# A selective-scan layer on one core: the input product of the scan as matmuls with diagonal blocks, and plain additions of y

## What is computed

```
dA  = jnp.exp(dt[..., None] * A)
dBx = (dt * x)[..., None] * Bm[:, :, None, :]
def step(h, inputs):
    dA_t, dBx_t, C_t = inputs
    h = dA_t * h + dBx_t
    y = jnp.einsum('bdn,bn->bd', h, C_t)
    return (h, y)
...
y = ys + x * D
```

## Time and profile before

| | us |
|---|---|
| median of 3 runs | 1387.32 |
| lowest, highest | 1381.39, 1389.28 |
| the profiled execution | 1389.91 |
| its span, first to last instruction | 1388.1 |
| TensorE busy | 1228.0 (88%) |
| VectorE busy | 899.6 (65%) |
| GpSimd busy | 918.5 (66%) |
| ScalarE busy | 777.4 (56%) |

### The profile page before, as it was taken

The page is one execution under the profiler, slowest core; times in us unless marked ns, Lnnn a source line. Parts: engine busy times, 40 slices in busy tenths (PEclk is TensorE's granted clock), DMA queues, the critical chain, the costliest instruction groups (busy, mean ns, idle before and its releaser), DMA issues. The chain is left out here.

```text
span 1388.1 us, 20902 instructions
## 1 busy us (share of the span) xinstructions
PE 1228.0 (88%) x7120; PEld 933.0 (67%) x7120; DVE 899.6 (65%) x1065; ACT 777.4 (56%) x1477; POOL 918.5 (66%) x511
## 2 busy tenths in 40 slices
PE   8978878989788879797787879898999999999997
PEld 3445555656556556566556644467999999999996
DVE  3998999899899899899998889963111111111110
ACT  4787887788887697788886675613111111111111
POOL 1998999999999989999998879822222222222211
PEclk9999999999999899899998799999999999999999
DMA  5665556465556455556555554608988898888982
GB/s 196 216 182 183 168 184 176 156 202 192 176 171 198 152 184 165 183 171 192 186 184 182 178 155 152 194 4 301 369 309 322 318 322 313 310 320 317 323 306 46
DMA packets 109979, 296.95 MB, mean 214 GB/s; under 512 B 10017, under 2 KB 21922, under 8 KB 94386
## 3 DMA queue, kind: packets, MB, share of 16 engines
q1 hardware_dynamic: 100226, 277.53, 57.9%
q0 software_dynamic: 9648, 18.09, 6.5%
HBM read 277.76 MB, written 9.96 MB: 207 GB/s over the span
## 5 line engine op out<-in xcount | busy, mean ns | idle before, releaser
L1376 POOL TENSOR_TENSOR arena<-arena 128x1024 f32<-128x1024 f32 x192 | 456.7, 2395 | 53.8 <-DVE arena L1096 38.2
L472 PE MATMUL ps_y<-ident,arena 128*128 128x128 f32 x1840 | 258.5, 289 | 54.0 <-POOL arena L1376 53.3
L472 PEld LDWEIGHTS ps_y<-ident,arena 128*128 128x128 f32 x1840 | 222.2, 148 | 121.8 <-POOL arena L1376 74.3
L1428 POOL DMA_INDIRECT out_x<-arena x39 | 61.8, 1585 | 304.9 <-ACT arena L1024 279.8
L871 ACT ACTIVATE arena<-arena,An 128x512 f32<-128x512 f32 x316 | 218.6, 710 | 0.1
L871 ACT ACTIVATE ps_de<-arena,An 128x512 f32<-128x512 f32 x196 | 134.9, 688 | 146.4 <-DVE arena L1083 140.4
L1310 DVE TENSOR_TENSOR arena<-ps_du,arena 128x512 f32<-128x512 f32 x39 | 27.0, 692 | 227.8 <-PE ps_du L720 227.8
L1360 POOL TENSOR_TENSOR arena<-arena 128x1024 f32<-128x1024 f32 x67 | 160.2, 2391 | 6.7 <-DMA arena<-bc_scratch 6.7
L720 PE MATMUL ps_y<-arena 128*128 128x128 f32 x1248 | 153.4, 276 | 0.8 <-ACT arena L1012 0.5
L720 PEld LDWEIGHTS ps_y<-arena 128*128 128x128 f32 x1248 | 149.6, 193 | 3.2 <-ACT arena L1012 0.8
L1068 DVE TENSOR_TENSOR ps_u<-ps_du,arena 128x512 f32<-128x512 f32 x196 | 136.8, 698 | 22.2 <-DVE arena L1108 10.1
(11 more groups left out here) (238 smaller groups left out, 2009.2 us busy)
## 6 DMA issues: line engine op xcount, KB each, us to landing
arena<-bc_scratch SPq DMA_DIRECT2D x256, 512.0 KB, 4.7
arena<-in_W SPq DMA_DIRECT2D x117, 1024.0 KB
arena<-arena POOLq DMA_DIRECT2D x15, 512.0 KB, 6.0
arena<-in_cd SPq DMA_DIRECT2D x16, 256.0 KB, 5.4
out_x<-arena SPq DMA_DIRECT2D x17, 128.0 KB, 5.0
arena<-in_xT SPq DMA_DIRECT2D x2, 1024.0 KB, 6.3
arena<-in_w2c SPq DMA_DIRECT2D x1, 2048.0 KB, 9.2
diag<-in_dd SPq DMA_DIRECT2D x16, 128.0 KB, 5.1
```

The costliest lines, as they stand in the source:

```text
L472: t = e.matmul(Y[j][:, part], src[:, part], ident[:, :], start=False, stop=stop, is_transpose=True, skip_group_check=True)
L1376: e.tensor_tensor(hc[:, i % NP, :, :], hh[:, i % NH, :, :], c, ALU.mult).then_inc(gp_hc, 1)
L1428: e.indirect_dma_start(out, bass.IndirectOffsetOnAxis(dest[:, i:i + 1], 0), yo[:, i % 3, :], None, compute_op=ALU.add).then_inc(l_add, 16)
```

## The change

From unit 16 on, the input u of both scans is made by TensorE alone. For each unit the 512 values of B[n] are laid out as four diagonal blocks of 128x128; a product of the transposed du (stationary) with such a block (moving) gives du · B in PSUM, where both scans read it. The diagonals are built in a DRAM scratch: it is zeroed once (16 transfers), and for each half sequence four transfers write single elements at a stride of 513. Then the loads of B read the blocks (256 KB a unit, as the spread rows did). Decays then all go to SBUF. In the first 16 units u is made as before by VectorE and GpSimd, now in all of them. Own units become 3, 7, 11 and 15 of the first 16, and 4, 12, 20 and 28 of each 32 after. All additions to Y become matmuls of 128x512 against the identity, and with them the products with D and of the forward direction; nothing is turned back. The ring of three pairs becomes six buffers for B and six for C. Slots of the side work are moved by some units.

```diff
-OWN = (6, 9, 12, 15, 22, 25, 28, 31)
-NR, NH, NP, KD, LAG, EV, NW = 3, 5, 4, 6, 2, 4, 3
+FIRST = 16
+OWN_FIRST, OWN = (3, 7, 11, 15), (4, 12, 20, 28)
+NRB, NRC, NH, NP, KD, LAG, EV, NW = 6, 6, 5, 4, 6, 2, 4, 3
...
+DU_AT = {16 * g - 5 + j + (3 if g == 1 else g == 7): (g, j) for g in range(1, 16) for j in range(2)}
+SCATTER_AT = {i_: (0, 0, k) for k, i_ in enumerate((7, 8, 9, 10))}
+SCATTER_AT |= {22 + k: (0, 1, k) for k in range(4)}
+SCATTER_AT |= {32 * c_ - 12 + 2 * k: (c_ // 2, c_ % 2, k) for c_ in range(2, 2 * NQ) for k in range(4)}
+ZERO_AT = {i_: (c_, 2 * k) for c_ in range(2) for k, i_ in enumerate(range(12 * c_, 12 * c_ + 8))}
...
+        S = [[DU, DE[0]], [U, DE[1]]]
...
                 for j in range(2):
-                    t = add_blocks(q, th, j, hc[:, i % NP, j, :], n == 15)
+                    t = e.matmul(Y[j][:, :], ident[:, :], hc[:, i % NP, j, :], start=False, stop=(n == 15))
                 t.then_inc(pe_y, 1)
...
+            def make_u(i):
+                g, k_ = i // 16, i - 2
+                if i == FIRST:
+                    e.wait_ge(dv_u, FIRST)
+                e.wait_ge(dv_sA, k_ + 1)
+                e.wait_ge(dv_sB, k_ + 1)
+                if own(k_):
+                    e.wait_ge(dv_hc, owned(k_))
+                for j in range(2):
+                    is_free(("du", g, j))
+                rb_has(e, i)
+                for j in range(2):
+                    for k in range(4):
+                        t = e.matmul(S[i % 2][j][:, QUARTERS[k]], duT[:, g % 2, k, j * 128:j * 128 + 128],
+                                     rb[:, i % NRB, QUARTERS[k]], start=True, stop=True)
+                t.then_inc(pe_u, 1)
 
             for i in range(NU + LAG):
-                if i + 1 in DU_AT:
-                    turn_inputs(i + 1)
...
+                if FIRST <= i < NU - 2:
+                    if i == FIRST:
+                        make_u(i)
+                        make_u(i + 1)
+                    make_u(i + 2)
                 if i < NU:
                     side_work(i)
...
-                decay, x = (h[:, 1, :], DE[i % 2][:, :]) if flipped(i) else (DE[i % 2][:, :], h[:, 1, :])
+                decay, x = (DE[i % 2][:, :], h[:, 1, :]) if i < FIRST else (h[:, 1, :], S[i % 2][1][:, :])
...
+            def load_b(i):
...
+                if i < FIRST:
+                    src = bc_dram[0:1, n, HB[0]].to_broadcast([128, TH])
+                else:
+                    src = dg_dram[th, n, 0:128 * TH].rearrange("(p t) -> p t", t=TH)
+                e.dma_start(rb[:, i % NRB, :], src).then_inc(l_rb[i % NRB], 16)
...
+            def put_diagonals(q, th, k):
...
+                to = dg_dram[th].rearrange("n (p f) -> n p f", f=TH + 1)[:, :, k * 128]
+                src = xd[RK:RK + NS, th * TH + k * 128:th * TH + k * 128 + 128]
+                e.dma_start(to, src, allow_slow_non_contiguous=True).then_inc(l_dg, 16)
...
             for i in range(NU):
...
-                if not flipped(i):
+                if i < FIRST:
                     u(i)
...
-                if swapped(i):
-                    first_scan(i)
-                    second_scan(i)
-                else:
-                    second_scan(i)
-                    first_scan(i)
+                second_scan(i)
+                first_scan(i)
```

More of the change, by code:

```diff
@@ L73 @@
+TILE_AT = {at(2, 46): (0, 4), at(2, 47): (0, 5), at(2, 54): (0, 6), at(2, 55): (0, 7),
+           at(3, 6): (0, 0), at(3, 7): (0, 1), at(3, 14): (0, 2), at(3, 15): (0, 3),
+           at(3, 46): (1, 4), at(3, 47): (1, 5), at(3, 51): (1, 6), at(3, 52): (1, 7)}
 TILES = list(TILE_AT.values()) + [(1, i) for i in range(4)]
 TILE_NO = {x: k for k, x in enumerate(TILES)}
[L77 to L84, removed]
@@ L87, in plain @@
[L87 to L104, removed]
+DU_AT = {16 * g - 5 + j + (3 if g == 1 else g == 7): (g, j) for g in range(1, 16) for j in range(2)}
+CD_AT = {(slots[2 * m] - 4 if m < 2 else slots[2 * m - 3] + 7): (q_, m) for q_, slots in CONV_SLOTS.items() for m in range(4)}
@@ L253, in build @@
         pe_D, ac_ev = (sem(n) for n in ("D", "ev"))
-        ac_yT, pe_back = sem("yT"), sem("back")
-        pe_dT, pe_bT, ac_uT, pe_u1, pe_u0, ac_kept = (sem(n) for n in ("dT", "bT", "uT", "pu1", "pu0", "kept"))
+        pe_u = sem("pu")
         ac_z = sem("z")
@@ L283, in own, with rb_has, rc_has, made @@
         def own(i):
-            return i % 32 in OWN
+            return i in OWN_FIRST if i < FIRST else i % 32 in OWN
         def owned(i):
-            return i // 32 * len(OWN) + sum(k <= i % 32 for k in OWN)
+            return sum(own(k) for k in range(i + 1))
+        def rb_has(e, i):
+            e.wait_ge(l_rb[i % NRB], 16 * (i // NRB + 1))
+        def rc_has(e, i):
+            e.wait_ge(l_rcs[i % NRC], 16 * (i // NRC + 1))
+        def made(i):
+            return i - FIRST + 1
+        def cd_of(q, m):
+            return duT[:, 1, :, :].rearrange("p k (a f) -> p k a f", a=2)[:, :, m % 2, :] if q == 0 and m >= 2 else cdiag[:, m % 2, :, :]
+        def du_of(g):
+            return du1 if g == 1 else duA
         def cols_of(q, th):
@@ L458, in tile_lg @@
                 e.matmul(PS[p][:, 0:E], ones_r, bgr, start=False, stop=True).then_inc(pe_lg, 1)
[L460 to L474, removed]
             def first_sum(i, j):
@@ L480, in first_sum @@
                     qe, the, pre, _ = unit(i - 16)
-                    if turned(qe, the):
+                    if qe == 3 and the:
+                        e.wait_ge(dv_lg, 2 * pre + j + 1)
+                    else:
                         e.wait_ge(ac_ev, nth_sum(qe, the, 2 * pre + j))
-                    else:
-                        e.wait_ge(dv_lg, 2 * pre + j + 1)
                 e.wait_ge(l_D, 16 * (i // 16 + 1))
                 has_x(e, q, m, th)
[L487 to L493, removed]
+                e.matmul(Y[j][:, :], diag[:, j, :], xc[q % 2][:, m, HB[th]], start=True, stop=False).then_inc(pe_D, 1)
             def add(i):
                 q, th, pr, n = unit(i)
-                if n == 0 and i >= 16 and turned(*unit(i - 16)[:2]):
-                    turn_back(i)
                 for j in range(2):
@@ L613, in second_u @@
[L613 to L622, removed]
-                    e.wait_ge(dv_hc, owned(i - 1))
-                for k in range(4):
-                    t = e.transpose(U[:, QUARTERS[k]], uT[:, k, 0:128], ident[:, :])
-                t.then_inc(pe_u0, 1)
@@ L897, in evac_turned @@
                     is_full(e, ("wb", NB - 1))
+                    if pr:
+                        for j in range(2):
+                            is_full(e, ("du", 1, j))
                 elif q == 2:
```

317 lines of the change are left out of this document (150 added, 167 removed).

## The result

| | before | after |
|---|---|---|
| median, us | 1384.36 | 1781.42 |
| lowest to highest, us | 1381.12 to 1389.28 | 1780.01 to 1787.78 |
| span of the profiled execution, us | 1388.1 | 1778.1 |
| last addition to y ends, us | 915.75 | 1308.43 |
| behind it, us | 472.3 | 469.7 |

The ratio is 1.287, with an interval of 1.282 to 1.293. The kernel is slower by 397 us. Of the 390.0 us between the two profiled spans, all lies ahead of the last addition (392.7 us later); the part behind it is the same within 3 us. The forecast was 1722 us in a range of 1690 to 1810; the time lies in the range, 59 us above the forecast.

The account below looks back on a forecast made before the run. The loop, paced by VectorE and GpSimd before, was to become bound by TensorE: 427 + 416 + 289 = 1132 us from 96 us, ending 312 us later; 1389.9 + 312 + 22 - 2.6 gave 1722 us, range 1690 to 1810.

Parts of the forecast that it names:

- TensorE's two new terms: Per loop unit on TensorE: make_u 1.78 us plus plain additions to y 1.72 us, 3.50 us before any other work.
- the signs that it named: Profile after: TensorE busy 97% or more, VectorE and GpSimd idle a third, units 4.7 us on average, clock near 1.0.
- The price of make_u and of the additions: On TensorE, 1.78 us a unit for eight make_u matmuls, 1.72 us for two addition matmuls, both recorded twice per matmul.
- 4× faster for FP32: Skill's factor for transposes on TensorE; as a rival it put make_u at 3.52 us and the time at 2140 us, chance 0.01.
- The start of the saturated part: First make_u, at unit 16, starts near 96 us, after 52.5 us of TensorE work counted from 43.2 us.
- rival 1: Scattered diagonal writes: hidden at 51 ns a packet, 140 us more at 128 ns, so 1862 us; chance 0.07.
- 22 us: Allowance of 2% of TensorE's 1132 us for edges, zeroing of scratch at the start and moments at the lower clock.
- TensorE's work from there on: Loop from 96 us: make_u 427, additions 416 and side work 289 us, 1132 us if TensorE never waits.
- The upper price: TensorE's records priced by busy time over count: 1239 us of loop work, 107 more, 1806 us without the allowance.
- rival 3: TensorE at the upper price, from intermittent waits or a lower clock: 1770 to 1810 us, chance 0.10.
- Rival 2: One record for each TensorE matmul, make_u 0.9 and an addition 0.86 us, VectorE then binding: 1208 us, chance 0.02.
- point of decision: One-record rival decides once TensorE's unit is below 3.44 us: the two terms below 2.2 us with 1.2 us side work.

Follow-up runs that it names:

- e1: Kernel before with only the additions to y, products with D and forward sums as plain matmuls, nothing turned back, u made as before: 1407.3 us.
- e2 to e4: Changed kernel with make_u as transposes, multiplication with B left out (1619.2 us); with the additions turned as before (1668.9 us); with both edits (1542.9 us).
- e8: Changed kernel without scratch traffic (no zeroing, no diagonals written, plain rows of B loaded) and with make_u as transposes: 1530.2 us.
- e6: Changed kernel with each diagonal write made as 16 contiguous pieces instead of 2048 single elements, zeroing and loads kept: 1759.8 us.
- e7: Changed kernel without zeroing, diagonal writes and the waits for them, loading plain rows of B for all units: 1750.7 us.
- e5: Changed kernel without VectorE's own products past the first group, GpSimd making all of them there: 1778.5 us.
- e10: Changed kernel without scratch traffic, with make_u as transposes and the additions turned as before: 1417.8 us.

## Why the prediction was right, and where it was off

**What bounds the loop: right.** The forecast said that TensorE's two new terms exceed a whole unit of before (3.50 against 3.44 us), that VectorE and GpSimd then idle, and that the clock is full. The stage from 200 us on shows all three. e1 and e2 to e4 show it by changing parts: the additions alone go into TensorE's idle time and cost 23 us; in the changed kernel the saved records give back 162 and 112 us. Of the signs that it named, TensorE's share came out at 96% and not 97, VectorE and GpSimd idle half of the loop and not a third, and a unit takes 1173.6/240 = 4.89 us on average and not 4.7.

**The price of make_u and of the additions: right.** 1.79 and 1.71 us against 1.78 and 1.72. The row of the same shape in another stage was the right one to take. The Trainium skill's "4× faster for FP32" (TensorE: Matmul & The Clock Gate, Terms) was set against it; e8 saved 220 us for 1920 matmuls, 0.115 us each. By a factor of four the ordinary matmul would have to cost 0.33 us more than its transpose, and the saving would be some 630 us. So the measurement speaks for a factor of two here.

**The start of the saturated part: mis-sized by 39 us.** The forecast put make_u(16) at 96 us, and it starts at 134.9. The step that failed is rival 1's. Its price per packet was right (50 ns against 51 in the row). But it was weighed only for the later half sequences, with units of 4.7 us, four writes in eight units and loads five units ahead, and only by the time of the 16 DMA engines, not by what stands behind a write on SyncE's queue. The first four writes stand in units 7 to 10, one after another, where units last some 3 us and 8 MB of zeros are being written. For the start the forecast named only "the zeroing of scratch" within its 22 us, and put the scattering there at nothing. Without the scattering (e6) make_u(16) starts 24.9 us earlier, without the rest of the scratch traffic (e7) another 9.0, and 5.0 of the 39 stay unexplained.

**TensorE's work from there on: 42 us more than 1132.** The loop takes 1308.43 - 134.86 = 1173.6 us. TensorE's waits in the whole execution:

```profile
PE ps_du L595 <- DVE ps_du L1041: 9.2, 5, 1.9
PE ps_du L595 <- issue: 4.7, 3, 3.8
PE ps_du L595 <- DMA arena<-dg_scratch: 2.7, 1, 2.7
...
PE ps_u L595 <- issue: 2.1, 3, 1.0
```

These are 18.7 us of waiting in front of make_u, in a queue that by the count never waits. The forecast had weighed make_u's wait for the scans only; in an own unit it also waits for VectorE's product with C, and those are the 9.2 us that are gone in e5. The second part is the edges of odd shapes. A unit with one step width:

```profile
155.81 1.05 PE L595 MATMUL ps_u<-arena 128*128 128x128 f32 x8
156.70 1.06 PE L595 MATMUL ps_de<-arena 128*128 128x128 f32 x8
157.69 1.12 PE L386 MATMUL ps<-arena,dtT 16*128 16x512 f32 x2
158.74 1.99 PE L491 MATMUL ps_y<-arena,ident 128*128 128x512 f32 x4
160.56 1.05 PE L595 MATMUL ps_du<-arena 128*128 128x128 f32 x8
```

From 155.81 to 160.56 us it takes 4.75 us; 3.50 + 0.86 = 4.36 was counted. The matmul with 16 rows takes 1.05 instead of 0.86 us, and the groups before and behind it 0.1 us more each. So a step width costs 0.39 us more, 28 of them 11 us. The matmuls of x_rows (L364, the rows of B and C, 48 columns of weights) cost 0.33 us more for each group of four records; 14 groups make 4.6 us. With convolution, gates and projections no such edge shows. The third part is the clock behind the longest waits (2.7 us at 191 us, 3.8 and 1.9 us at 1236 and 1253 us):

```profile
180.00:200.00 20.00, 17.29 (x71) 10.91 (x70) 9.00 (x9) 8.70 (x16) 9.51 (x5) 0.91 0.71 182
...
1256.00:1258.00 2.00, 2.00 (x10) 1.91 (x10) 1.43 (x3) 0.00 (x0) 1.10 (x1) 0.50 0.00 0
```

It is 0.91 from 180 to 200 us and from 1240 to 1260 us, with 0.50 (1.2 GHz) in the two microseconds shown, and 1.00 in all other stretches of 20 us from 140 to 1300. That makes 2 x 20 x 0.09 = 3.6 us. The sum is 18.7 + 15.5 + 3.6 = 38 of 42 us; the rest is not separated. The allowance of 22 us was meant for all of this and the start.

Together: 39 + 42 - 22 = 59 us, which is the miss.

**The upper price, 1806 us**, came nearer than the forecast (25 us off against 59), but not by its sum: the cost of a record was the low one, and the clock full from 200 us on but for the stretches named. The time also lies outside the 1690 to 1770 us that had a chance of 0.79, and inside rival 3's 1770 to 1810, which had 0.10. Rival 3 was to come "from intermittent waits or a lower clock". Intermittent waits are what happened (the 28.9 us of stalls before unit 16 and the 18.7 us of make_u), with a lower clock behind them (0.66 from 80 to 100 us, 0.72 from 100 to 120 us), but the rival gave no place or price for them. So that the time lay in the range is in part luck.

**Rival 2** (one record everywhere) was put at 1208 us. e10 is that case but for the side work, whose matmuls keep two records, and stands at 1417.8 us, 2.5% above the kernel before (1.022 to 1.028). The rival's point of decision was that a gain comes once the two terms are below 2.2 us with side work of 1.2 us. In e10 they are 1.8 us by the count (0.89 each), and still the time is not below that of before. So that point was too high; the gaps and the lower clock above stood in its place. With single records in the side work too the time could be lower; no run tried it, and the rival's number is not shown either way.

**Smaller misreadings.** "91 to 98%" and "82 to 87%" hold for the stages that were shown up to 600 us; from 600 to 800 us TensorE was busy 80%, and from 800 to 914 us TensorE 89%, VectorE 90% and GpSimd 82%. The sum of the forecast gives 1721, not 1722. Neither changes the argument.

## What to carry to other kernels

Before work is moved to an engine with idle time, add up that engine's whole unit at start-to-start prices, from a stretch where its queue is full and with the same shapes; here 3.50 us before any side work against a unit of 3.44 decided at once. Count a plain float32 matmul as two records and a transpose as one (0.22 and 0.11 us for 128 columns here), and expect that an edit that fits into idle time alone doesn't once the engine is full (the plain additions cost 23 us alone and 112 to 147 us on top of make_u). A transfer of single elements has to be weighed where units are shortest and loads least ahead, and what waits behind it, on its queue and on others, counts, not its bytes. And a gap in TensorE's queue costs more than its length where the clock falls behind it.

## What the runs showed of the hardware

Three of the first four DMAs of 2048 single elements (8 KB) held the next DMA instruction of their queue for 8.7 to 10.1 us, though at 50 ns a packet over 16 engines their packets take 6.4 us; the other 29 held it for 0.3 to 8.0 us. A transfer of GpSimd's queue in the same stretch was waited for 12.5 us, and 4.1 us without the single elements. A float32 matmul with only 16 rows took 0.19 us more than one of 128 rows, and the groups beside it 0.1 us each; those with all rows and columns had no such cost. After waits of 3.8 us (at 1236 us) and 1.9 us (at 1253 us) TensorE's granted clock was 0.50 from 1256 to 1258 us, where it is 1.00 through the stretches without gaps.
